# A selective-scan stage whose logarithm correction moves from VectorE to ScalarE and GpSimd, with new instruction orders on four engines

## What is computed

```python
xn = layernorm(layernorm(h))               # the residual is h + layernorm(h)
x_main, z = split(xn @ W_in.T)
x_main = silu(causal_conv4(x_main) + conv_b)
Bt, Ct = x_main @ W_B.T, x_main @ W_C.T    # 16 states
dt = softplus(x_main @ W_dt.T + b_dt)
dA = exp(-exp(log_A) * dt);  dBx = dt * Bt * x_main
h_t = dA_t * h_(t-1) + dBx_t               # a scan over 3138 tokens
y = sum over states (h * Ct)
h = h + layernorm(h) + (y * silu(z)) @ W_out.T
```

## Time and profile before

| | |
|---|---|
| median of 3 executions | 2622.25 us (2622.24 to 2623.73) |
| profiled execution: its time, its span | 2624.39 us, 2622.6 us |
| busy over the span: PE, DVE, ACT, POOL | 2268.7, 2223.6, 1628.2, 2124.0 us |
| stage A | from the start to about 1440 us |
| instructions | 26642 |

### The profile page before, as it was taken

One profiled execution on the slowest core, in us unless ns is written; L12 is line 12 of the kernel. 1 busy time (PEld: TensorE's weight loads), 2 busy tenths in 40 slices (PEclk: granted clock), 3 DMA queues, 4 the chain that ended last, 5 costly groups with the idle time before them and its releaser, 6 DMA issues. The chain is left out here.

```text
span 2622.6 us, 26642 instructions
## 1 busy us (share of the span) xinstructions
PE 2268.7 (87%) x6899; PEld 1114.1 (42%) x6899; DVE 2223.6 (85%) x3592; ACT 1628.2 (62%) x3076; POOL 2124.0 (81%) x1135
## 2 busy tenths in 40 slices
PE   5999999999999999999997118843899999999998
PEld 2444444444444444444443113321455555555544
DVE  2999999999999999999997772214799998999985
ACT  4787877887887887887873204424555565555543
POOL 2999999999999999999996017876788788888862
PEclk8999999999999999999998559875899999999999
DMA  2243343343343343343342203330011111111100
GB/s 79 91 123 114 98 125 112 99 125 111 99 127 110 100 126 109 104 127 105 102 125 59 83 9 65 67 36 25 25 39 39 33 37 33 33 33 33 38 27 18
DMA packets 180611, 199.45 MB, mean 76 GB/s; under 512 B 40062, under 2 KB 170988, under 8 KB 180332
## 3 DMA queue, kind: packets, MB, share of 16 engines
q1 hardware_dynamic: 169196, 189.35, 23.8%
q0 software_dynamic: 11264, 8.40, 2.4%
HBM read 164.44 MB, written 33.25 MB: 75 GB/s over the span
## 5 line engine op out<-in xcount | busy, mean ns | idle before, releaser
L914 POOL TENSOR_TENSOR a_hc<-a_h,a_cs 128x896 f32<-128x896 f32 (+1 forms) x448 | 861.7, 1945 | 30.1 <-PE a_y_bank L362 16.1
L362 PE MATMUL a_y_bank<-a_hc,a_ident 128*128 128x448 f32 (+1 forms) x1792 | 755.9, 547 | 38.9 <-POOL a_hc L914 33.3
L553 ACT ACTIVATE a_da<-a_dt,a_neg_a 128x448 f32<-128x448 f32 (+1 forms) x896 | 549.9, 631 | 195.2 <-DVE a_h L784 192.8
L784 DVE TENSOR_TENSOR_SCAN a_h<-a_da,a_h,a_dbx 128x448 f32<-128x448 f32 x528 | 575.1, 1130 | 2.2
L362 PEld LDWEIGHTS a_y_bank<-a_hc,a_ident 128*128 128x128 f32 x1792 | 330.7, 191 | 356.4 <-issue 255.9
L1788 PE MATMUL c_p_E<-c_w_ex,c_hid 128*128 128x512 f32 x800 | 375.3, 603 | 19.0 <-DVE c_sc L2043 15.7
L2193 POOL TENSOR_TENSOR c_prod<-c_prob,c_qkv 128x1024 f32<-128x1024 f32 x100 | 281.0, 2838 | 117.2 <-DVE c_prob L2067 117.2
L768 DVE TENSOR_TENSOR a_dbx<-a_dtx,a_b_bank 128x896 f32<-128x896 f32 (+1 forms) x308 | 329.9, 1071 | 14.5 <-PE a_b_bank L355 13.8
L902 POOL TENSOR_TENSOR a_dbp<-a_dtx,a_bs 128x896 f32<-128x896 f32 (+1 forms) x140 | 272.2, 1944 | 0.1
L784 DVE TENSOR_TENSOR_SCAN a_h<-a_da,a_h,a_dbp 128x448 f32<-128x448 f32 x240 | 267.7, 1131 | 0.0
L2184 POOL TENSOR_TENSOR c_prod<-c_qkv 128x1024 f32<-128x1024 f32 x100 | 232.2, 2354 | 20.6 <-ACT c_qkv L1856 20.4
(11 more groups left out here) (310 smaller groups left out, 3678.0 us busy)
## 6 DMA issues: line engine op xcount, KB each, us to landing
a_cs<-c_rows SPq DMA_DIRECT2D x96, 896.0 KB, 5.3
a_bs<-c_rows SPq DMA_DIRECT2D x24, 1120.0 KB, 5.6
a_cs<-c_rows SPq DMA_DIRECT2D x16, 900.0 KB, 4.4
c_x<-h_rows SPq DMA_DIRECT2D x100, 64.0 KB, 2.2
...
```

Of the source, the lines that this page charges most:

```text
L362: pe.matmul(y_bank[:, d, 0:g.w], ident[:], hc[:, (g.i * NS + n) % HC_RING, d, 0:g.w], start=(n == 0), stop=(n == NS - 1)).then_inc(s_sum, 1)
L553: act.activation(da[:, k % DA_RING, 0:g.w], dt[g.slot][:, d, 0:g.w], ACT.Exp, scale=neg_a[:, d * NS + n:d * NS + n + 1]).then_inc(s_da, 1)
L784: dve.tensor_tensor_scan(h[:, n, d, 0:g.w], da[:, (g.i * 2 * NS + k) % DA_RING, 0:g.w], x, state, ALU.mult, ALU.add).then_inc(s_scan, 1)
L914: pool.tensor_tensor(hc[:, (q.i * NS + n) % HC_RING, :, 0:q.w], h[:, n, :, 0:q.w], cs[:, n % C_RING, 0:q.w].unsqueeze(1).to_broadcast([P, ...
```

## The change

The correction of the logarithm was one VectorE instruction (`lost`: (1 + e) - 1 - e). It becomes a pass on ScalarE (`one_less`: adds the column -1 to 1 + e) and a subtraction on GpSimd (`lost`, with its wait for `one_less`). The sum `kept` moves from GpSimd to VectorE. The lists of the four engines are written in another order, and the line of WORK_ORDER follows TensorE's list (`dt1` ahead of `bc`).

```diff
+            def one_less():
+                if p:
+                    act.wait_ge(s_spu, 2 * p.i + 1)
+                    act.activation(yt[:, :, 0:p.w], yt[:, :, 0:p.w], ACT.Identity, bias=eps_cols[:, 2:3]).then_inc(s_spu, 1)
...
     def vector(dve):
-            def lost():
-                if p:
-                    w = p.w
-                    dve.wait_ge(s_spu, p.i + 1)
-                    dve.scalar_tensor_tensor(out=yt[:, :, 0:w], in0=yt[:, :, 0:w], scalar=-1.0, in1=spe[:, :, 0:w],
-                                             op0=ALU.add, op1=ALU.subtract).then_inc(s_spd, 1)
+            def kept():
+                if f:
+                    dve.wait_ge(s_n1, f.i + 1)
...
+                    dve.tensor_tensor(hn[f.i % 3][:, 0:f.w], h0[:, 0:f.w], n1[:, 0:f.w], ALU.add).then_inc(s_hn, 1)
...
     def gpsimd(pool):
+            def lost():
+                if p:
+                    w = p.w
+                    pool.wait_ge(s_spu, 2 * p.i + 2)
+                    pool.tensor_tensor(yt[:, :, 0:w], yt[:, :, 0:w], spe[:, :, 0:w], ALU.subtract).then_inc(s_spd, 1)
...
             weigh(10)
+            lost()
             log_sum()
+            weigh(11)
             steps()
-            weigh(11)
             weigh(12)
+            weigh(13)
             stepped()
-            weigh(13)
             weigh(14)
             next_product(3)
-            kept()
             weigh(15)
```

On TensorE the places that matter below are these; `b_row(5)` goes ahead of `gate(0)`, `b_row(13)` ahead of `variance_out`:

```diff
             sum_state(0)
+            b_row(5)
             gate(0)
-            b_row(5)
             gate(1)
+            b_row(7)
             step(0)
...
             sum_state(7)
             b_row(13)
+            variance_out()
             token()
```

More of the change, by code:

```diff
@@ L718, in scalar @@
             keep_b_and_c()
+            keep_rows()
+            log_of_sum()
             decays(9)
+            decays(10)
+            middle_b()
+            decays(11)
+            tail()
             one_more()
-            keep_rows()
-            middle_b()
+            low_b()
             square_out()
-            decays(10)
-            low_b()
-            decays(11)
-            positive()
-            scale_out()
-            log_of_sum()
-            decays(12)
-            keep_token()
-            decays(13)
+            one_less()
+            scale_out()
+            keep_token()
+            decays(12)
+            decays(13)
+            positive()
+            square()
             keep_logit()
-            square()
             decays(14)
-            tail()
             scales()
             decays(15)
+            affine()
             next_decays()
-            affine()
             keep_norm()
@@ L873, in vector @@
             scans(9, 1)
-            product(11)
             scans(10, 0)
             scans(10, 1)
+            product(11)
             scans(11, 0)
+            product(13)
+            normed_out()
             scans(11, 1)
-            lost()
-            normed_out()
             scans(12, 0)
-            product(13)
             scans(12, 1)
@@ L888, in vector @@
             scans(14, 1)
+            normed()
             scans(15, 0)
             scans(15, 1)
-            normed()
             normed_twice()
+            kept()
             next_product()
@@ L945, in stepped @@
                                        ).then_inc(s_dtx, 1)
-            def kept():
-                if f:
-                    pool.wait_ge(s_n1, f.i + 1)
-                    if f.i >= 3:
-                        taken(pool, "out", chunk(f.i - 3))
-                    pool.tensor_tensor(hn[f.i % 3][:, 0:f.w], h0[:, 0:f.w], n1[:, 0:f.w], ALU.add).then_inc(s_hn, 1)
+            def lost():
[3 more added lines that the diff above has]
+                    pool.tensor_tensor(yt[:, :, 0:w], yt[:, :, 0:w], spe[:, :, 0:w], ALU.subtract).then_inc(s_spd, 1)
             weigh(0)
             weigh(1)
+            product(6)
             weigh(2)
-            product(6)
             weigh(3)
+            weigh(4)
             product(9)
-            weigh(4)
             product(12)
```

37 lines of the change are left out of this document (19 added, 18 removed).

## The result

The changed kernel takes 2683.07 us (median of 4 runs, 2677.75 to 2684.22) against 2622.24 us for the kernel before (4 runs, 2620.12 to 2623.73) on the same chip: a ratio of 1.0231, 95% interval [1.0217, 1.0244]. It is slower, by about twice what I forecast (+61 us for +29), and outside my range. The profiled execution took 2682.88 us, its span is 2681.1.

The account below looks back on a forecast made before the run. VectorE was taken to set stage A's pace. A turn of 49.14 us would become 50.2 with the new waits, +1.05; 27.3 us over 26 turns plus some 2 gives +29, 2651 us, range 2605 to 2672.

Parts of the forecast that it names:

- `kept` into the last 0.5 us of `stepped`: End of turn: kept meets the last 0.4 us of GpSimd's stepped and waits 0.3 us; bounds 0 to 1.9.
- GpSimd's waits at 2.0 us a turn: Sign to look for in the timeline: GpSimd with about 2 us of waits a turn, more than now.
- Step 1: decays(5) behind biased(0) on ScalarE: VectorE waits 0.4 us before scan(5,0), giving back the time saved at product(7).
- TensorE's granted clock is 1.00: Read from stage A's steady part before the change: TensorE at its upper clock level, 2.4 GHz.
- step 2: normed_out behind a longer ScalarE list, through square_out, variance_out and scale_out: VectorE waits 1.0 us before normed_out.
- It doesn't set the pace: GpSimd as a bound: its turn comes to 49.0 us, below the forecast turn of 50.2, so it is not the bound.
- steps 1 to 3: VectorE's new waits: 0.4 us before scan(5,0), 1.0 before normed_out, 0.1 before scan(12,0), where the decay follows keep_token.
- The bare gain: VectorE's turn without new waits: 49.14 less net 0.46 (lost out, kept in) and 0.35 at product(7), giving 48.3 us.
- The 0.35 at `product(7)`: VectorE's wait of 0.27 us there, some 0.35 with restart, goes because b_row(7) now stands ahead of step(0).
- The 0.98 of `lost`: Time that lost costs VectorE each turn, saved when the correction leaves VectorE's list.
- kept is shut out for long: Rival: kept waits up to a whole GpSimd operation, 1.9 us instead of 0.3; +43 us, 2694 us; chance 0.10.
- its second form: Within the rival of a long shut-out: GpSimd's next operation goes ahead of the waiting kept; left open by the profile row.

Follow-up runs that it names:

- e6: The kernel before with only the head of TensorE's list in the new order and product(5) ahead of scans(4,0): ratio 1.0003, turns of 49.09 us.
- e1: The changed kernel with zero-adding products on TensorE at both idle places, ahead of variance_out and ahead of token: ratio 1.0148, turns of 50.5 us.
- e9: The changed kernel with two zero-adding products on TensorE ahead of variance_out only: ratio 1.0139, no half-clock stretch.
- e10: The changed kernel with three zero-adding products on TensorE ahead of token only: ratio 1.0134, no half-clock stretch.
- e11: The changed kernel with the middle of the turn reordered on ScalarE and TensorE (square_out, low_b ahead of decays(11)): ratio 1.0138, turns of 50.46 us.
- e12: e11 with TensorE fed zero-adding products at both idle places, and kept given one SBUF input and put ahead of normed_twice: ratio 1.0116, turns of 50.10 us.
- e14: e11 with the first half of GpSimd's list in the order of before: ratio 1.0118, turns of 50.22 us.
- e15: e12 with the first half of GpSimd's list in the order of before: ratio 1.0081, turns of 49.87 us.
- e17: e15 with stepped ahead of weigh(13) on GpSimd: ratio 1.0070, turns of 49.78 us.
- e13: The changed kernel with the first half of GpSimd's list in the order of before: ratio 1.0263, turns of 50.54 us without a half clock.
- e5: The kernel before with only the correction moved to ScalarE and GpSimd, kept staying on GpSimd: ratio 1.0214, turns of 50.15 and 51.85 us.
- e2: The changed kernel with one_more, square_out, one_less moved on ScalarE and variance_out ahead of sum_state(7) and b_row(13) on TensorE: ratio 1.0302, turns of 52.02 us.
- e4: The kernel before with only kept moved to VectorE, behind normed_twice: ratio 1.0054, turns of 49.60 us.
- e3: The changed kernel with kept back on GpSimd at its old place: ratio 1.0187, turns of 50.16 us without a half clock.

## Why the prediction was half right

**The direction and the waits.** The steps that lay rows end to end around the scans held: 1.00 at `normed_out` (forecast 1.0), 0.1 ahead of scan(12,0) (0.1), `kept` into the last 0.5 us of `stepped` with 0.4 of standing (0.4 and 0.3), GpSimd's waits at 2.0 us a turn (about 2, though it was 1.95 before, and so not more), a turn of 50.52 (50.2). Step 1 had the wait too large, 0.17 us at `scan(5,0)` for 0.4, and the gain ahead of it too, since 0.10 stay at `product(7)` (as in e6): scan(5,0) comes 0.20 later than before, and 0.15 was forecast. The 0.3 by which the turn is longer than 50.2 are the stand ahead of scan(11,0), which no step had (0.17), `kept` (0.1 more) and this 0.05. So instead of the 27.3 us that I booked for the 26 turns, the turns without a half clock account for 26 x 1.38 = 36.

**The step that failed first: "TensorE's granted clock is 1.00".** I read it in the earlier trace rows and used TensorE's durations of before throughout, though by my own step 2 TensorE would stand and wait for `square_out` and for `scale_out`. I laid out that chain and asked only when it ends, not what TensorE does meanwhile. The nine stretches lengthen nine turns by 25.8 us in sum; e1, e9 and e10 remove them and leave the other turns as they are. With the 36, the 2 at the start and the 7 given back behind stage A's turns that is 57 of the 58.5 us between the two spans. My 50.2 us for every turn left out every term of this kind, and no rival had it.

**The step that failed second: "It doesn't set the pace"** (GpSimd, 49.0 us). I compared sums of work. But the waits in GpSimd's list don't vanish, since they hang on scans and on sums that close loops through the other engines: the 1.14 us for `lost` went, and 1.97 us of waits stand in the turn all the same, for 1.95. As I read the runs, the turn is held by such loops: a scan or a sum of TensorE releases a `weigh`; GpSimd runs from there to `stepped` without a gap, with `lost` new in it; `kept` is shut out until then, or `next_product` waits; then come the scans up to the one that released. The wait at `normed_out` lies in a loop of its own of nearly the same length. This would be why each cure gave so little. Taking 0.77 off the wait at `normed_out` gave 0.06 (e11). Opening `kept`'s exclusion then gave 0.36 (e12, and 0.35 from e14 to e15; these two also feed TensorE and move `kept` ahead of `normed_twice`); GpSimd's head 0.24 (e14) and 0.23 (e15); `stepped`, 0.09 (e17). Together 0.74 of the 1.38 us. In the changed kernel itself the head alone gave 0 (e13), for GpSimd then waited 0.26 us at `lost`, for `one_less`, and this ties it to the same ScalarE list. The two changes together gave 0.30 (e14), where each alone gave 0.06 and 0, as two loops of one length would; but I had expected 49.1 to 49.6 of cutting both and got 50.22, so they are not the whole, and the account by loops is argued and not shown. What is shown is that neither wait was "the" bound, and my attribution of the turn to the waits of steps 1 to 3 was wrong although its sum was close.

**The bare gain.** The 48.3 us a turn did not come in any run. The 0.35 at `product(7)` measured 0.06 (e6), since scan(4,1) holds it there too. The 0.98 of `lost` was cover for `log_of_sum` in the old order (e5). The new order keeps that from showing, but needs the longer stretch on ScalarE in the middle that makes step 2.

**The rivals.** "kept is shut out for long" turned up where the timing shifted it: 2.36 us in the long turns and 2.09 in e2, but never for longer than one GpSimd operation. Of its second form, GpSimd's next one going first, there is one trace: in the changed kernel's turn at 929.61 `kept` was issued with 0.05 us of a `weigh` to run and 0.01 ahead of the record of the next operation, and stood until that one's end (2.42 us). Otherwise it was the next GpSimd operation that took longer (2.33 us for 1.93 behind `kept`). e4's half per cent agrees with the 0.45 us that `kept` adds to each of its turns.

**Left open.** Of the 1.38 us, 0.64 remain in e17: its waits on VectorE sum to 0.93 us, 0.56 more than before, at six places for two, and an instruction behind a wait also loses the 0.08 or so by which it overlaps the one before. I haven't taken them away one by one. Nor do the runs say which idle time makes the clock fall: e11 has 1.07 us ahead of `token` in every turn and e2 1.69 us ahead of `variance_out`, and both keep the full clock; the kernel before has 0.59 us and 1.17 us at other places of each turn and keeps it too; the changed kernel has 0.47 and 0.72 and falls in nine turns of 26, e3 has the same two and falls in 15.
